# First layer of a two-layer graph network: the next adjacency tile prepared ahead of a tile's sums

## The reference

```
h  = relu(layernorm(x))
x1 = x + GNN0(h, adj)          # 4-bit quantised h, 3-bit quantised weight:
                               #   S = quant(relu(hq @ Wq)); out = adj @ S (scaled)
X  = relu(layernorm(x1))       # input of the second layer
R  = (adj + I) / rowsum(adj + I)
for s in 0, 1:                 # second layer
    A  = softmax(top_p_0.9(Xa W1 W2 (Xa W3)^T))
    Xf = R @ Xf;  Xa = A @ Xa
    Z += Xf @ U1[s] + Xa @ U2[s]
out = x1 + layernorm(X + Z) * gamma + beta
```

## Time and profile before

| | us |
|---|---|
| median of 3 runs (1460.14 to 1462.3) | 1460.16 |
| the profiled execution | 1462.12 |
| its span | 1460.3 |
| TensorE busy | 1217.0 (83%) |
| VectorE busy | 1098.2 (75%) |
| ScalarE busy | 611.0 (42%) |
| GpSimd busy | 292.6 (20%) |
| preamble, to the first adjacency product | 0 to 80.6 |
| first layer | 80.6 to about 371 |
| second layer | about 371 to 1460 |

### The profile page before, as it was taken

The page is one execution under the profiler, slowest core; times in us unless marked ns, Lnnn a source line. Parts: engine busy times, 40 slices in busy tenths (PEclk is TensorE's granted clock), DMA queues, the critical chain, the costliest instruction groups (busy, mean ns, idle before and its releaser), DMA issues.

```text
span 1460.3 us, 18002 instructions
## 1 busy us (share of the span) xinstructions
PE 1217.0 (83%) x6042; PEld 591.4 (40%) x6042; DVE 1098.2 (75%) x1864; ACT 611.0 (42%) x1164; POOL 292.6 (20%) x236
## 2 busy tenths in 40 slices
PE   0658888887779989989989999879999849689792
PEld 0324443443224445445445545424445325345351
DVE  7877666663389899869959800079999999999958
ACT  1635343332771255465544334494046236243130
POOL 6024333332022211121121210101111101102111
PEclk9989999998889999999999999989999979889996
DMA  6134444441214410020030040153440210111165
GB/s 218 49 132 169 166 168 151 173 152 60 88 51 154 156 44 30 32 85 15 31 101 16 30 166 15 45 208 103 157 137 30 66 51 29 66 51 44 44 225 178
DMA packets 57395, 141.78 MB, mean 97 GB/s; under 512 B 9632, under 2 KB 9632, under 8 KB 53216
## 3 DMA queue, kind: packets, MB, share of 16 engines
q1 hardware_dynamic: 57312, 140.81, 27.8%
HBM read 89.67 MB, written 51.12 MB: 96 GB/s over the span
## 4 chain that ended last, share of the span: by engine, by line
PE 46%; DVE 22%; issue 11%; POOL 8%; ACT 8%; DMA 3%; SPq 1%; DVEq 1%; POOLq 1%; ACTq 0%
DVE WS L1382 7%; PE UB L675 6%; PE AB L830 4%; PE AB L778 4%; PE RB L830 4%; PE AB L665 3%; PE RB L675 3%; PE XB L675 3%; PE RB L778 2%; POOL Plz L529 2%; ACT E L1088 2%; POOL RT L565 2%; PE AB L833 2%; PE AB L780 2%; DVE w L1596 2%
## 5 line engine op out<-in xcount | busy, mean ns | idle before, releaser
L1382 DVE SCALAR_TENSOR_TENSOR WS<-E,g 128x2048 bf16<-128x2048 f32 x128 | 315.4, 2515 | 2.0 <-ACT E L1088 0.8
L1469 DVE TENSOR_REDUCE g<-E 128x1 f32<-128x2048 f32 x32 | 72.9, 2278 | 143.1 <-ACT E L1061 143.1
L684 PE MATMUL TB<-ident,E 128*128 128x128 f32 x512 | 81.2, 287 | 72.8 <-ACT turns L1125 45.1
L1125 ACT ACTIVATE turns<-TB 128x512 f16<-128x512 f32 x128 | 75.3, 594 | 155.0 <-PE TB L690 154.8
L830 PE MATMUL AB<-XR,turns 128*128 128x512 f16 x512 | 130.3, 401 | 0.0
L565 POOL TENSOR_TENSOR RT<-RT,AD 128x512 f32<-128x512 f32 x32 | 55.2, 1725 | 361.3 <-ACT RT L1100 361.3
L830 PE MATMUL RB<-XR,turns 128*128 128x512 f16 x512 | 121.0, 379 | 0.0
L778 PE MATMUL RB<-VR,AH 128*128 128x512 f16 x512 | 115.6, 385 | 0.0
L778 PE MATMUL AB<-VR,turns 128*128 128x512 f16 x512 | 114.1, 379 | 0.0
L684 PEld LDWEIGHTS TB<-ident,E 128*128 128x128 f32 x512 | 66.4, 148 | 98.8 <-issue 48.6
L1119 ACT ACTIVATE turns<-TB 128x512 f16<-128x512 f32 x128 | 75.4, 593 | 34.6 <-PE TB L684 34.6
(11 more groups left out here) (292 smaller groups left out, 2245.5 us busy)
## 6 DMA issues: line engine op xcount, KB each, us to landing
turns<-adj_parts SPq DMA_DIRECT2D x48, 512.0 KB, 3.8
E<-adjT SPq DMA_DIRECT2D x16, 1024.0 KB, 5.1
adj_parts<-turns SPq DMA_DIRECT2D x16, 1024.0 KB, 3.9
AH<-adj_parts SPq DMA_DIRECT2D x16, 512.0 KB, 3.7
z_d<-UO SPq DMA_DIRECT2D x31, 256.0 KB, 2.3
XR<-x SPq DMA_DIRECT2D x4, 1024.0 KB, 12.0
WS<-U SPq DMA_DIRECT2D x4, 1024.0 KB, 5.6
x_d<-E SPq DMA_DIRECT2D x16, 256.0 KB, 2.6
```

The costliest lines, as they stand in the source:

```text
L684: i = mm(bank[:, k * P:(k + 1) * P], src(k), ident32[:, :], is_transpose=True, start=(k == 0), stop=(k == KC - 1), skip_group_check=True)
L1382: return v.scalar_tensor_tensor(junk[t % 2], e, g4[:, k, t:t + 1], e, op, ALU.mult, accum_out=g4[:, F_, t:t + 1])
```

## The change

Nothing is computed differently. What is moved:

- VectorE and ScalarE prepare adjacency tile t+1 (sums, split, own_block; adj_hi) ahead of the chain of tile t. The key sums get two buffers.
- In ScalarE's tile, adj_hi(t+1) stands before the copy of the transposes, and x_hi moves from the end of the tile to between UO and RT of post0.
- GpSimd does x_lo(t) before v_lo and pk_lo of t-1.
- SP's list of a tile becomes l0_stores(t), at_out(t+1), adj_in(t+3), diag_out(t), post0_stores(t-1).
- In the preamble: U10 is loaded before adjacency tile 0; GpSimd's u_lo(0) comes before all four ln_root; ScalarE's adj_hi(0) comes right behind u_hi(0); VectorE's sums of tile 0 stand before quantise_support(0), and wpk_parts (the split of the projection weights) before quantise_support(3).

```diff
@@ sync
-            sp.dma_start(raw[:, 0, :], adjT[0]).then_inc(s_raw, 16)
...
             u_in(0)
+            sp.dma_start(raw[:, 0, :], adjT[0]).then_inc(s_raw, 16)
             u_in(1)
...
+            def l0_tile(t, odd):
+                l0_stores(t)
+                at_out(t + 1, odd)
+                adj_in(t + 3)
+                diag_out(t)
+                post0_stores(t - 1)
+
             adj_in(1)
             u_in(2)
             at_out(0, 0)
+            adj_in(2)
             l0_stores(0)
+            at_out(1, 1)
+            adj_in(3)
+            diag_out(0)
             u_in(3)
-            for t in range(1, T - 1):
-                adj_in(t + 1)
-                at_out(t, t % 2)
-                diag_out(t - 1)
+            for t in range(1, T - 3):
+                l0_tile(t, (t + 1) % 2)
...
@@ gpsimd
-            ln_root(0)
-            ln_root(1)
             u_lo(0)
-            ln_root(2)
-            ln_root(3)
+            for b in range(NG):
+                ln_root(b)
             pool.wait_ge(s_sup, NG)
             u_lo(1)
...
             def l0_tile(t):
                 l0(t)
+                x_lo(t, of(XR, t))
                 v_lo(t - 1, of(VR, t - 1))
                 pk_lo(t - 1, 0, t - 1, s_vl, t)
-                x_lo(t, of(XR, t))
@@ tensor
-                mm(LB[0][:, 0:1], key_sums, powc[:, 1, 0:1], start=True, stop=True).then_inc(s_mm2, 1)
+                mm(LB[0][:, 0:1], key_sums[:, h, :], powc[:, 1, 0:1], start=True, stop=True).then_inc(s_mm2, 1)
@@ scalar
             u_hi(0)
+            adj_hi(0)
             for b in range(NG):
...
-            def post0(t):
+            def post0(t, more=True):
                 act.wait_ge(s_u, t + 1)
                 act.wait_ge(s_uout, 16 * t + OPEN)
                 a(UO[:, :], UB[:, :], ACT.Copy, scale=SV / (SX * SW)).then_inc(s_ue, 1)
+                if more:
+                    x_hi(t + 1)
...
             def l0_tile(t):
-                xT_halves(t - 1)
                 turn_free(t + 1)
                 adj_hi(t + 1)
+                xT_halves(t - 1)
                 post0(t - 1)
-                x_hi(t)
-
-            adj_hi(0)
...
@@ vector
+            def adj_sums(t):
+                dve.wait_ge(s_raw, 16 * t + 16)
+                v.tensor_reduce(key_sums[:, t % 2, :], raw[:, t % 2, :].rearrange("p (j c) -> p c j", j=T), AX.X,
+                                ALU.add).then_inc(s_part, 1)
+
+            quantise_x(0)
+            quantise_x(1)
+            adj_sums(0)
+            quantise_support(0)
+            quantise_x(2)
+            quantise_support(1)
+            quantise_x(3)
+            quantise_support(2)
+            wpk_parts(ch)
+            quantise_support(3)
+            adj_lo(0)
...
             def own_block(t, ct):
 
+                dve.wait_ge(s_diag, t)
...
-            def layer0(t, first=False):
+            def layer0(t, last=False):
                 ct = Chain(dve, c_dve, t * per0 + base)
-                adj_lo(t)
-                own_block(t, ct)
-                if first:
-                    wpk_parts(ct)
+                if not last:
+                    adj_sums(t + 1)
+                    adj_lo(t + 1)
+                    own_block(t + 1, ct)
                 dve.wait_ge(s_mm2, t + 1)
...
+            own_block(0, ch)
+            base = ch.n
+            with dve.Fori(0, T - 1) as t:
                 layer0(t)
```

More of the change, by code:

```diff
@@ L176, in build @@
         misc = E[:, 6, :].rearrange("p (a d) -> p a d", a=4)
-        X1T, tmp, key_sums, own = misc[:, 0, :], misc[:, 1, :], misc[:, 2, 0:P], misc[:, 2, P:2 * P]
+        X1T, tmp, own = misc[:, 0, :], misc[:, 1, :], misc[:, 2, 2 * P:3 * P]
+        key_sums = misc[:, 2, 0:2 * P].rearrange("p (h c) -> p h c", h=2)
         to_round = VR[:, :, :, :].rearrange("p t h d -> p t (h d)").bitcast(F32)
@@ L312, in _ @@
             at_out(0, 0)
+            adj_in(2)
             l0_stores(0)
+            at_out(1, 1)
+            adj_in(3)
+            diag_out(0)
             u_in(3)
-            for t in range(1, T - 1):
-                adj_in(t + 1)
-                at_out(t, t % 2)
-                diag_out(t - 1)
+            for t in range(1, T - 3):
+                l0_tile(t, (t + 1) % 2)
+            for t in range(T - 3, T - 1):
+                l0_stores(t)
+                at_out(t + 1, (t + 1) % 2)
+                diag_out(t)
                 post0_stores(t - 1)
-                l0_stores(t)
-            at_out(T - 1, 1)
-            diag_out(T - 2)
+            l0_stores(T - 1)
             post0_stores(T - 2)
-            l0_stores(T - 1)
             post0_stores(T - 1)
@@ L971, in support_rounded, with adj_hi @@
                 a(sup[:, tiles, :], to_round[:, tiles, :], ACT.Copy, bias=-ROUND).then_inc(s_sup, 1)
+            def adj_hi(t):
+                act.wait_ge(s_raw, 16 * t + 16)
+                a(turns[:, t % 2, 0, :, :].rearrange("p t c -> p (t c)"), raw[:, t % 2, :], ACT.Copy,
+                  scale=SA).then_inc(s_ah, 1)
             u_hi(0)
+            adj_hi(0)
             for b in range(NG):
@@ L983, in _ @@
                     support_rounded(b - 1)
[L985 to L988, removed]
             def turn_free(t):
@@ L1052, in _ @@
             post0(T - 2)
-            x_hi(T - 1)
             xT_halves(T - 1)
-            post0(T - 1)
+            post0(T - 1, False)
             def logits_out(qq, slot, chunks=range(NC)):
@@ L1297, in quantise_support @@
                     v.tensor_scalar(sup[:, tiles, :], u, ROUND, None, ALU.subtract).then_inc(s_sup, 1)
[L1299 to L1317, removed]
             def wpk_parts(ct):
@@ L1328, in wpk_parts, with adj_lo @@
                     v.tensor_tensor(WPK[:, :, 1, c], src, WPK[:, :, 0, c], ALU.subtract).then_inc(s_wpk, 1)
+            def adj_sums(t):
+                dve.wait_ge(s_raw, 16 * t + 16)
+                v.tensor_reduce(key_sums[:, t % 2, :], raw[:, t % 2, :].rearrange("p (j c) -> p c j", j=T), AX.X,
+                                ALU.add).then_inc(s_part, 1)
+            def adj_lo(t):
+                dve.wait_ge(s_ah, t + 1)
+                v.scalar_tensor_tensor(turns[:, t % 2, 1, :, :].rearrange("p t c -> p (t c)"), raw[:, t % 2, :], SA,
+                                       turns[:, t % 2, 0, :, :].rearrange("p t c -> p (t c)"), ALU.mult,
+                                       ALU.subtract).then_inc(s_al, 1)
+            quantise_x(0)
[10 more added lines that the diff above has]
+            base = ch.n
+            per0 = 9
             def own_block(t, ct):
+                dve.wait_ge(s_diag, t)
                 ct(v.tensor_tensor(own, raw[:, t % 2, bass.ts(t, P)], ident32[:, :], ALU.add))
@@ L1360, in layer0 @@
                 v.tensor_scalar(XF[:, :], tmp, 0.0, SX, ALU.max, ALU.mult).then_inc(s_xf, 1)
[L1361 to L1366, removed]
+                assert ct.n == per0 - (3 if last else 1)
+            own_block(0, ch)
+            base = ch.n
+            with dve.Fori(0, T - 1) as t:
                 layer0(t)
                 v.tensor_copy(sc[:, 26:27], sc[:, 25:26]).then_inc(c_dve, 1)
+            dve.wait_ge(c_dve, base + per0 * (T - 1))
+            layer0(T - 1, True)
+            base -= 3
             base += per0 * T
```

## The result

| | before, us | changed, us |
|---|---|---|
| median of 4 runs | 1461.14 | 1409.57 (1407.79 to 1412.09) |
| span of the profiled execution | 1460.3 | 1408.4 |
| first layer, from the first adjacency product to the first logits product | 80.64 to 372.43 | 81.66 to 319.04 |
| TensorE busy | 83% | 85% |

Changed over before is 0.9648, 95% interval 0.963 to 0.9666: 51.6 us faster. 1415 was forecast, with a range of 1406 to 1431.

A forecast was written before the change was run, and what follows sets the result against it. TensorE nearly the bound, its two waits winnable: 238.4 - 14 x 13.95 - 5.4 = 37.7 us; with 3.0, 1.5 and 3.5, 45.7. Profiled 1462.1 becomes 1416.4, median 2.0 lower, 1414.5, said as 1415; range 1406 to 1431.

The forecast's parts named there:

- The two waits: TensorE, each first-layer tile: for VectorE's low half (1.15 us) and GpSimd's low half of the activations (1.40); both go.
- The ring over VectorE and ScalarE: Chain, x_hi, RT to pk, adj_hi, split, own_block and hand-overs: 13.0 us a tile, 0.95 under TensorE's 13.95.
- A: Rival: the ring across VectorE and ScalarE bounds the tile at 15.3 us; gain 32 us, 1428; chance 0.17.
- C: Rival: only the first wait goes, pk frees the bank as late as x_lo did; gain 19 us, 1441; chance 0.06.
- D: Rival: slower; VectorE's split and own_block collide with GpSimd passes each tile, ring 19.4 us; 1485; chance 0.05.
- The sum of 13.83: Steady tile: TensorE's own products and transposes together, without waits, in us.
- 13.95: Forecast steady tile in us, between TensorE's own 13.83 and 14.17, the old tile less its two waits.
- the preamble's 1.5 us: Before the first layer: U10's earlier load and GpSimd pass let VectorE start sooner; 1.5 us won, bounds 0 and 1.9.
- B: Rival: the waits go but clock dips stay, every third tile 1.0 us longer; gain 40 us, 1420; chance 0.10.
- Tiles 2 and 3: Once-only collisions with u_hi(3) and u_lo(3): waits of 3.1 us for XT and 2.3 before transposes; 5.4 lost.
- The first tile: X1 of tile 0 at 95.9, UB products of tile 1 at 105.8 against 108.83: 3.0 us won.
- The tail: Tile 15: transposes 2.5 us sooner, the UB products after them 1.0 faster; 3.5 us won.

The follow-up runs named there:

- u_lo(1) alone: Changed kernel with GpSimd's u_lo(1) waiting for own_block(0) instead of the support: 1409.32 us, ratio 0.9635.
- moving the other passes alone: Changed kernel with u_hi(2), u_hi(3), u_lo(2) and u_lo(3) moved from tiles 1 and 2 to the last two tiles: 1404.76 us, ratio 0.961.
- both together: Changed kernel with u_lo(1) behind own_block(0), the U20 and U21 splits in the last two tiles, and two roots ahead of u_lo(0): 1399.16 us, ratio 0.9572.

## Why the prediction was right

**The two waits and their cause: right.** Neither is left in a steady tile. The experiments show that both orders are needed: with one alone a wait of 0.73 or 1.14 us is left. SP's new order cost nothing, as forecast: between 95 and 340 us no engine waits for an adjacency load.

**What bounds then: right.** TensorE is busy for 160.08 of 160.08 us. The ring over VectorE and ScalarE is shorter, but close: VectorE waits 0.27 for the key sum, where 0.6 was forecast. Rivals A, C and D did not come; the split takes 2.29 and own_block's last instruction 0.29.

**The size of a tile: wrong by 0.61, the largest error.** The term "transposes 0.94" in TensorE's own row of work was read from a tile in which they stood behind a wait, where they are slow; without the wait they take 0.44. The sum of 13.83 becomes 13.33, and the measured 13.34 lies outside the 13.8 to 14.2 that the prediction named as its sign of being right. And 13.95 was chosen above that sum for fear that part of the gap to 14.17 stays; it was drain, and all of it went. Over 14 tiles the two make 8.5 us, more than the whole miss in the median (1415 against 1409.57). That the miss is no larger is luck: the preamble's 1.5 us did not come, and the clock behind the first layer took another 1.5. The clock gave no further surprise: B was wrong too, and with either wait gone the dips are gone.

**The once-only terms.** Tiles 2 and 3: 5.4 forecast, 5.9 measured (138.41 - 105.80 - 2 x 13.34), the first as a wait of 2.84 for XT behind u_hi(3) and adj_hi(3), as described. The second was forecast as a wait of 2.3 ahead of the transposes of tile 2, and here only the number came out: from the UB products of tile 2 (122.80) to those of tile 3 (138.41) 15.61 us pass, 2.27 more than 13.34, of which 1.65 are the UB products themselves, partly at half clock (4.45 instead of 2.75), and the rest is slow transposes (0.95) with hardly any wait. The slow UB products moved the time at which the transposes are due, and pk(1) ended 0.6 sooner than forecast (134.6 for 135.2). The first tile: X1 ready at 96.7, where 95.9 was forecast, or 94.4 with the preamble's term; the own_block behind GpSimd's pass took 4.15 as forecast. The UB products of tile 1 start at 105.80, where 105.8 less 1.5 was forecast.

**The preamble: wrong in sign at its end.** Forecast 1.5 sooner, measured 1.0 later (81.66 against 80.64). GpSimd's part held: u_lo(0) starts 2.4 sooner (27.12 for 29.54), where 2.6 was forecast, and ends at 31.2. The step that failed is "VectorE starts up to 1.9 us sooner": the pass stood in the way of the statistics of the last group, which the prediction had free of GpSimd, and VectorE starts 0.6 later (34.53 for 33.95). The sums then did not fit whole into the wait of 2.79: the third group is quantised from 53.23 instead of 51.97, 1.3 later. How much of the 1.0 at the end is scatter stays open, and the effect of the whole preamble is under what the runs can tell.

**The tail: 3.5 forecast, 4.65 measured.** The transposes start 7.9 us behind the UB products, as forecast (8.0); that is 2.95 sooner than before. They are fast there (0.62 for 1.01, which ran at a granted clock of 0.50), and the UB products behind them took 4.39, where 5.30 stood before: the clock gave 1.3 us in UB and RB, where 1.0 was forecast.

## What to carry to other kernels

A wait on a nearly full TensorE costs more than its idle time: here each one also cost 0.16 to 0.17 us of drain, one made the looped transposes behind it 0.5 us slower, and with two in a tile the granted clock fell to 0.90 in every third tile. So durations of instructions behind a wait are not those that they have once the wait is gone; look for the same instructions elsewhere in the trace without one. Work of the next tile belongs ahead of the chain that waits for this one's end, and large once-only passes belong where the ring's engines have a gap, which the timeline shows: here that brought another 10 us. And an edit that wins nothing alone can be worth its full price once the next wait behind it is gone: u_lo(1) alone won nothing that shows, and moving the other passes alone 4.8 us, but both together 10.4.

## What the runs showed of the hardware

Eight transposes with addresses from a loop variable take 0.95 us behind a wait and 0.44 without one, while the same eight with fixed addresses take 0.44 behind a wait too. A 128x4 instruction of VectorE stood for 3.75 us beside a GpSimd pass of 4.06, and a 128x128 one with two inputs in SBUF for 4.15, while a reduction of 128x2048 beside the same kind of pass kept its 3.67. It went the other way too: the GpSimd pass that began 0.16 us behind VectorE's split of 2.29 took 6.04 instead of 4.08. The Trainium skill (GPSIMD Engine Reference, Specifications) says that GpSimd shares its SBUF interfaces with VectorE, and contends with instructions that have two SBUF inputs or run in a 2-port mode. The trace agrees for the 128x128 instruction, which has two such inputs, and for the reduction, which has one; the 128x4 one has one as well, and whether it ran in a 2-port mode no row shows.
